# Moving the low-part subtractions of the context blocks from GpSimd to VectorE

## The chip, the cores and the metric

The kernel runs on one core of a Trainium2 chip. The time is the device time of one execution in microseconds. Engines are TensorE (PE in the profile; PEld is its weight load), VectorE (DVE), ScalarE (ACT), GpSimd (POOL) and SyncE (SP), which issues the DMAs.

## What is computed

A block of a perceiver: a cross-attention of 128 latent rows per batch (4 batches) over 2048 context rows each, then a recurrent block with ternary weights, then a mixture of 8 experts. Only the first part is touched:

```python
x = x + xattn(layernorm(x), ctx, bias, Wq, Wk, Wv, Wo)
# xattn, 16 heads of depth 32:
q = heads(x @ Wq) * 32 ** -0.5
k = heads(ctx @ Wk)
v = heads(ctx @ Wv)
out = softmax(q @ k.T + bias) @ v      # then @ Wo
```

## The kernel before, in words

The products with Wk and Wv are made in split precision. A context block `ctx_raw` (512 channels x 512 context rows, 1 MB, held as 128 x 2048 elements) is cast into a high part and a low part, both in `ctx_part`: high = cast(raw), low = raw - high. A product then takes three matmuls: high x high, high x low and low x high (L340 to L342 for keys, L361 to L363 for values). The high part is made by ScalarE (L684), the low part by a subtraction of 128 x 2048 elements.

The attention goes over 16 quads (a batch and four heads each) in 4 blocks of 32 latent rows, 64 *turns* s = 0 to 63. Meanwhile the context is visited: a visit projects one block into keys or values, in four parts, one visit per turn, turns 0 to 59. Visits 0 to 3 are done ahead of turn 0, visit s + 4 in turn s. Three buffers hold context blocks; 27 visits of `FRESH[1:]` need a newly loaded one. The visits 1 to 3 have their low part made by VectorE ahead of turn 0, the other 24 by GpSimd. `highs_after` sets the turn: the cast of a block is made behind part 2 (`HIGH_AT`) of the visit that follows the last use of its buffer, and its first reader comes two turns after the cast. This gives one subtraction in each of the turns 1, 5, 9, 10, 11, 12, 13, 17, 21, 25, 26, 27, 28, 29, 33, 37, 41, 42, 43, 44, 45, 49, 53 and 57.

What a turn does, by engine, each in this order:

- TensorE: 32 score matmuls (L438), three parts of the visit, the spread of the masked minima (L449, waits for VectorE's mask), the fourth part; in every fourth turn, from turn 4 on, also the product of the finished quad with V (L461, 128 matmuls, waits for `shift` of this turn) and the folding of the sums (L469). The scores of turn s + 1 need the four bias-adds of turn s.
- VectorE: four bias-adds with a running minimum (L565), the mask (L579, 128 x 16), the transposition of the previous turn's probabilities (L574), the reduction `shift` (L586, waits for the spread). Then, in turns 0 to 12, the sums of two weight pieces of the later ternary stage (L603, up to 128 x 1024 each), and in 26 of the turns from 14 to 55 the scaling of one piece (L627 and L630). Turns 27, 35, 39 and 43 have the pieces of 768 columns. In the turn behind a product, VectorE first inverts the sums and scales the output (L591, L598).
- ScalarE: copies of finished projections (L690, L698), the cast of a context block (L684), four exponentials (L731, wait for `shift`), the ternary conversion (L741).
- GpSimd: only the subtractions (L799), each waiting for its cast.
- SyncE: loads and stores in program order; a context block is loaded when the visit that freed its buffer is done.

Each engine works strictly in the order of its program; semaphores join them.

Of the kernel before, what the change touches and what calls it, by code (L numbers as in the profile page):

```python
# [9 lines left out]
F32 = mybir.dt.float32  # L10
# [4 lines left out]
ALU = mybir.AluOpType  # L15
# [17 lines left out]
CHUNKS = KEYS // CHUNK  # L33
# [37 lines left out]
def place_visits():  # L71

    chunk = [(h // 2, c) for kind, h, c in VISITS]
    held, used, buffer_of, fresh, freed_by = [None] * BUFFERS, [None] * BUFFERS, [], [], {}
    for i, one in enumerate(chunk):
        if one not in held:
            until = [chunk.index(other, i) if other in chunk[i:] else len(chunk) for other in held]
            at = min(range(BUFFERS), key=lambda n: (-until[n], -1 if used[n] is None else used[n]))
            fresh.append(i)
            freed_by[i] = used[at]  # L80
            held[at] = one
        at = held.index(one)
        used[at] = i
        buffer_of.append(at)
    return buffer_of, fresh, freed_by


BUFFER_OF, FRESH, FREED_BY = place_visits()
# [54 lines left out]
def perceiver_block(nc, a, out):  # L143
    with ExitStack() as life:
        def sb(name, shape, dt, stack=life):
            return stack.enter_context(nc.sbuf_tensor(name, shape, dt))

        def sem(name):
            return life.enter_context(nc.semaphore(name))

        def events(name, keys, by=1):
            return Events(sem(name), list(keys), by)
# [30 lines left out]
        ctx_raw = sb("ctx_raw", [P, BUFFERS, 2, DT, CHUNK], F32, region_i)  # L183
# [5 lines left out]
        ctx_part = sb("ctx_part", [P, BUFFERS, 2, DT, CHUNK], F32R, region_r)  # L189
# [40 lines left out]
        quads, turns = range(QUADS), range(QUADS * BLOCKS)  # L230
# [20 lines left out]
        slice_low = events("slice_low", [*((part, k) for k in range(DT) for part in ("wk", "ctx")),  # L251
                                         *(("wv", k) for k in range(DT))])
        ctx_high = events("ctx_high", FRESH[1:])
        ctx_low_v, ctx_low_g = events("ctx_low_v", FRESH[1:CHUNKS]), events("ctx_low_g", FRESH[CHUNKS:])
        key_order = [(h, c, m) for h in range(STAGES) for c in range(CHUNKS) for m in range(2)]
        value_order = [(h, c, pair) for h in range(STAGES) for c in reversed(range(CHUNKS)) for pair in range(2)]
        keys_projected, keys_copied = events("keys_projected", key_order), events("keys_copied", key_order)
# [21 lines left out]
        top_out = psum[:, 7, 2 * P:2 * P + RANGES * QUAD].rearrange("p (a j) -> p a j", a=RANGES)  # L279
        mean_out = psum[:, 7, 3 * P:3 * P + len(TERNARY)]  # L280

        def ctx_low(i):
            return (ctx_low_v if i < CHUNKS else ctx_low_g).at(i)

        def wait_for_ctx(pe, i):
            if i in FRESH:
                pe.wait_ge(*ctx_low(i))

        def visit_done(i):

# [3 lines left out]
        def parts_of(s):  # L294

            first = sum(PARTS) * (s // BLOCKS) + sum(PARTS[:s % BLOCKS])
            parts = [divmod(CHUNKS * PARTS_OF_VISIT + p, PARTS_OF_VISIT) for p in range(first, first + PARTS[s % BLOCKS])]
            return [(i, r) for i, r in parts if i < len(VISITS)]

        def highs_after(i, r):  # L300

            return [fresh for fresh in FRESH if FREED_BY[fresh] == i - 1 and r == HIGH_AT]

        def quad_weighed_in(s):

            return s // BLOCKS - 1 if s % BLOCKS == 0 and s >= BLOCKS else None
# [9 lines left out]
        def pieces_summed_in(s):  # L316
            return [u for u in (2 * s, 2 * s + 1) if 0 <= u < len(TERNARY)]
# [199 lines left out]
        def vector_attention(dve):  # L517
            own = vector_own

            def low_of_ctx(i):  # L520
                dve.wait_ge(*ctx_high.at(i))
                buffer = BUFFER_OF[i]
                dve.tensor_tensor(ctx_part[:, buffer, 1, :, :], ctx_raw[:, buffer, 1, :, :],
                                  ctx_part[:, buffer, 0, :, :].bitcast(F32),
                                  ALU.subtract).then_inc(*ctx_low_v.made(i))

            def normalise_x():
                rstd = scalars("rstd0")
# [30 lines left out]
            def add_bias(s, j):  # L559
                if (s, j) == (0, 0):  # L560
                    dve.wait_ge(*bias_placed.at(RANGES - 1, BLOCKS - 1))
                if s >= 2 and j == 0:
                    dve.wait_ge(*transposed.at(s - 2))
                dve.wait_ge(*scored.at(s, j))
                dve.tensor_tensor_reduce(  # L565
                    places_of(s)[:, j, :], psum[:, j, :], biasmap[:, (s % BLOCKS) * BANK:(s % BLOCKS + 1) * BANK], 1.0,
                    HIGHEST, ALU.add, ALU.min, top[:, s % 2, j:j + 1]).then_inc(*biased.made(s, j))

            def transpose_turn(s):
                n, block = divmod(s, BLOCKS)  # L570
                dve.wait_ge(*raised.at(s))
                if block == 0 and n:
                    dve.wait_ge(*multiplied.at(n - 1))
                dve.transpose(probT[:, :, block, :],  # L574
                              places_of(s).rearrange("p j (k r) -> p (j k) r", r=DH)).then_inc(*transposed.made(s))
# [8 lines left out]
            def join_ranges(s):  # L584
                dve.wait_ge(*top_spread.at(s))
                dve.tensor_reduce(shift[:, s % 2, :], top_out.rearrange("p a j -> p j a"), AX.X,  # L586
                                  ALU.min).then_inc(*least_made.made(s))

            def invert_sums(n):
                dve.wait_ge(*sums_folded.at(n))  # L590
                dve.reciprocal(inverse[:, :], sums_out).then_inc(*own.made())  # L591

            def finish(n):
                dve.wait_ge(*own.last())
                if n >= 1:
                    dve.wait_ge(*attended_stored.at(n - 1))
                last = attended_sb[:, DT - 1, (B - 1) * P:B * P]
                dve.tensor_tensor(oT[:, :] if n < QUADS - 1 else last, quad_out, inverse[:, :],  # L598
                                  ALU.mult).then_inc(*weighted.made(n))
# [60 lines left out]
            for s in turns:  # L660
                n = quad_weighed_in(s - 1)
                if n is not None:
                    invert_sums(n)
                    finish(n)
                for j in range(QUAD):
                    add_bias(s, j)
                mask_top(s)
                if s:
                    transpose_turn(s - 1)
                join_ranges(s)  # L670
                for u in pieces_summed_in(s):
                    sum_weights(u)
                if s == MEAN_AT:
                    find_means()
                if piece_scaled_in(s) is not None:
                    scale_weights(piece_scaled_in(s))
# [96 lines left out]
        def gpsimd_attention(pool):  # L773
            own = gpsimd_own
            pool.memset(ident[:, :], 0.0).then_inc(*own.made())
            pool.wait_ge(*own.last())
            pool.affine_select(out=ident[:, :], in_=ident[:, :], compare_op=ALU.not_equal, fill=1.0, base=0,
                               pattern=[[-1, P]], channel_multiplier=1).then_inc(*constants.made("ident"))
            pool.wait_ge(*constants.at("ident"))
            pool.memset(ones[:, :], 1.0)  # L780
            pool.memset(magic[:, 0:1], ROUND_MAGIC)
            pool.memset(magic[:, 1:2], -ROUND_MAGIC)
            pool.memset(minus_half[:, :], -0.5).then_inc(*constants.made("all"))
            pool.wait_ge(*constants.at("all"))
            for k in range(DT):
                pool.wait_ge(*slice_in[k].at("ctx"))
                pool.tensor_copy(ctx_part[:, 0, 0, k, :], ctx_raw[:, 0, 1, k, :]).then_inc(*first_ctx_high.made(k))
            rstd = scalars("rstd0")
            for t in range(B):
                pool.wait_ge(*row_measured.at(0, t))  # L790
                pool.tensor_scalar(rstd[:, t:t + 1], meanvar[:, t, 1:2], 1.0, 1e-5, ALU.mult,
                                   ALU.add).then_inc(*own.made())
                pool.wait_ge(*own.last())
                pool.tensor_tensor(rstd[:, t:t + 1], rstd[:, t:t + 1], minus_half[:, 0:1],
                                   ALU.pow).then_inc(*row_rooted.made(0, t))
            def low_of_ctx(i):
                pool.wait_ge(*ctx_high.at(i))
                buffer = BUFFER_OF[i]
                pool.tensor_tensor(ctx_part[:, buffer, 1, :, :], ctx_raw[:, buffer, 1, :, :],  # L799
                                   ctx_part[:, buffer, 0, :, :].bitcast(F32),  # L800
                                   ALU.subtract).then_inc(*ctx_low_g.made(i))

            for s in turns:
                for i, r in parts_of(s):
                    for fresh in highs_after(i, r):
                        low_of_ctx(fresh)


        def sync_attention(sp):
# [1817 lines left out]
```

## Time and profile before

| what | us |
|---|---|
| median of 3 runs | 983.29 |
| lowest and highest run | 980.52 and 991.42 |
| the profiled execution | 979.04 |
| its span in the trace | 976.6 |
| TensorE busy | 911.2 (93%) |
| VectorE busy | 623.5 (64%) |
| ScalarE busy | 502.1 (51%) |
| GpSimd busy | 215.2 (22%), of it 111.1 in L799 |

The turns lie between about 52 and 593 us of the span. Busy times are those of the one profiled execution; its own time is 2.4 us longer than its span. A busy share is an average over the whole kernel: VectorE's 64% is 84% between 100 and 200 us and 69% between 500 and 600.

### The profile page before, as it was taken

What the parts mean: (1) busy time and instruction counts of PE and PEld (TensorE: products, weight loads), DVE (VectorE), ACT (ScalarE), POOL (GpSimd) and SP (SyncE); (2) the same over time, 40 slices, a digit from 0 to 9 for tenths busy, and PEclk for the clock granted to TensorE, in tenths of its full rate; (3) what the DMA queues carried; (4) which work ended last, traced back from release to release, by engine and by line L of the source; (5) the groups of instructions that cost most, each with busy time, mean ns of one, the idle gap of its engine ahead of it and who ended that gap; (6) DMA issues with size and microseconds to landing.
All of it is one profiled execution on the core that took longest, in us unless ns stands there. A gap on an engine that the chain in (4) does not pass through costs nothing.

```text
span 976.6 us, 22422 instructions
## 1 busy us (share of the span) xinstructions
PE 911.2 (93%) x9506; PEld 750.4 (77%) x9506; DVE 623.5 (64%) x1256; ACT 502.1 (51%) x988; POOL 215.2 (22%) x216
## 2 busy tenths in 40 slices
PE   7999999999988999989999957878999999999996
PEld 5888786886866887877887833644799999999995
DVE  6379987786786678677677666775651112566551
ACT  3545666565684566675457534688410102455551
POOL 2010135011063011151101102688110201111100
PEclk8999999999998999999999978999899999999999
DMA  9435374213352113451140471000099947899930
GB/s 331 142 131 171 121 255 166 93 66 131 109 193 77 48 61 104 156 177 43 58 133 34 129 283 69 6 1 12 34 370 386 371 159 265 287 380 345 340 86 14
DMA packets 76173, 154.73 MB, mean 158 GB/s; under 512 B 5416, under 2 KB 9000, under 8 KB 75552
## 3 DMA queue, kind: packets, MB, share of 16 engines
q1 hardware_dynamic: 73952, 148.40, 43.7%
q0 software_dynamic: 2112, 4.80, 2.1%
q8 instruction: 77, 1.26, 0.5%
q14 instruction: 32, 0.26, 0.1%
HBM read 140.24 MB, written 11.90 MB: 156 GB/s over the span
## 4 chain that ended last, share of the span: by engine, by line
PE 79%; DVE 9%; POOL 5%; issue 3%; DMA 3%; SPq 0%; ACT 0%; POOLq 0%; DVEq 0%; ACTq 0%
PE psum L2031 12%; PE psum L438 7%; PE psum L340 6%; PE psum L461 6%; PE psum L361 6%; PE psum L2046 6%; PE psum L342 6%; PE psum L341 6%; PE psum L362 5%; PE psum L363 5%; DVE prob L565 3%; PE psum L2063 2%; PE psum L2065 2%; PE psum L2064 2%; DVE probT L574 1%
## 5 line engine op out<-in xcount | busy, mean ns | idle before, releaser
L731 ACT ACTIVATE prob<-prob,shift 128x512 f32<-128x512 f32 x256 | 181.8, 712 | 88.9 <-DVE shift L586 88.9
L565 DVE CUSTOM_DVE_ANT_0 prob<-psum,biasmap 128x512 f32<-128x512 f32 x256 | 161.7, 686 | 67.6 <-PE psum L438 67.3
L799 POOL TENSOR_TENSOR ctx_part<-ctx_raw,ctx_part 128x2048 fp32r<-128x2048 f32 x24 | 111.1, 4630 | 423.0 <-ACT ctx_part L684 423.0
L361 PE MATMUL psum<-wv_hi,ctx_part 128*128 128x256 f32 x512 | 150.7, 294 | 0.0
L574 DVE STREAM_TRANSPOSE probT<-prob 128x2048 f32<-128x2048 f32 x64 | 147.4, 2303 | 0.7 <-ACT prob L731 0.5
L362 PE MATMUL psum<-wv_lo,ctx_part 128*128 128x256 f32 x512 | 144.8, 283 | 0.8 <-issue 0.8
L363 PE MATMUL psum<-wv_hi,ctx_part 128*128 128x256 f32 x512 | 144.6, 282 | 0.0
L2031 PE MATMUL psum<-xT,wring 128*128 128x128 f32 (+3 forms) x1024 | 134.0, 291 | 0.4 <-ACT xT L2385 0.4
L2031 PEld LDWEIGHTS psum<-xT,wring 128*128 128x128 f32 x1024 | 130.4, 191 | 1.8 <-ACT xT L2385 0.7
L361 PEld LDWEIGHTS psum<-wv_hi,ctx_part 128*128 128x128 f32 x512 | 97.8, 191 | 26.8 <-issue 26.0
L340 PE MATMUL psum<-ctx_part,wk_hi 128*128 128x512 f32 x248 | 104.8, 423 | 0.4 <-issue 0.4
L342 PE MATMUL psum<-ctx_part,wk_lo 128*128 128x512 f32 x248 | 99.3, 400 | 0.0
L341 PE MATMUL psum<-ctx_part,wk_hi 128*128 128x512 f32 x248 | 99.3, 400 | 0.0
L362 PEld LDWEIGHTS psum<-wv_lo,ctx_part 128*128 128x128 f32 x512 | 98.0, 191 | 1.0 <-issue 1.0
L363 PEld LDWEIGHTS psum<-wv_hi,ctx_part 128*128 128x128 f32 x512 | 97.9, 191 | 0.0
L438 PE MATMUL psum<-keys_and_values,q_all 32*32 32x512 f32 x2048 | 79.2, 613 | 5.3 <-issue 5.3
L698 ACT COPY keys_and_values<-psum 128x512 f32<-128x512 f32 x64 | 36.8, 576 | 70.5 <-PE psum L363 70.5
L340 PEld LDWEIGHTS psum<-ctx_part,wk_hi 128*128 128x128 f32 x248 | 48.0, 194 | 32.2 <-issue 23.8
L690 ACT COPY keys_and_values<-psum 128x512 f32<-128x512 f32 x64 | 36.8, 577 | 67.7 <-PE psum L342 67.7
L2267 DVE TENSOR_SCALAR hidden<-psum,b 128x128 f32<-128x128 f32 (+3 forms) x64 | 23.5, 368 | 74.6 <-PE psum L2031 74.4
L461 PE MATMUL psum<-probT,keys_and_values 128*32 128x128 f32 x2048 | 62.6, 283 | 2.3 <-DVE shift L586 2.3
L461 PEld LDWEIGHTS psum<-probT,keys_and_values 128*32 128x32 f32 x2048 | 58.2, 114 | 7.4 <-DVE probT L574 3.8
(258 smaller groups left out, 1429.0 us busy)
## 6 DMA issues: line engine op xcount, KB each, us to landing
wring<-in_w SPq DMA_DIRECT2D x64, 1024.0 KB, 8.1
ctx_raw<-in_ctx_t SPq DMA_DIRECT2D x27, 1024.0 KB, 5.2
raw_piece<-in_w_gate_t SPq DMA_DIRECT2D x16, 512.0 KB, 4.1
ternary_weights<-ternary_piece SPq DMA_DIRECT2D x21, 256.0 KB, 2.2
raw_piece<-in_w_down_t SPq DMA_DIRECT2D x10, 512.0 KB, 5.0
raw_piece<-in_w_gate_t SPq DMA_DIRECT2D x8, 384.0 KB, 4.0
ternary<-ternary_weights SPq DMA_DIRECT2D x1, 2816.0 KB, 9.5
raw_piece<-in_w_i_t SPq DMA_DIRECT2D x4, 512.0 KB, 5.4
```

The lines of the kernel that those rows point to most:

```text
L340: pe.matmul(psum[:, w, :], wh, ctx_part[:, BUFFER_OF[i], 0, k, :], start=(k == 0), stop=False)
L341: pe.matmul(psum[:, w, :], wh, ctx_part[:, BUFFER_OF[i], 1, k, :], start=False, stop=False)
L342: mm = pe.matmul(psum[:, w, :], wl, ctx_part[:, BUFFER_OF[i], 0, k, :], start=False, stop=(k == DT - 1))
L361: pe.matmul(place, keys_of(0, k), wv_hi[:, k, columns], start=(k == 0), stop=False)
L362: pe.matmul(place, keys_of(0, k), wv_lo[:, k, columns], start=False, stop=False)
L363: mm = pe.matmul(place, keys_of(1, k), wv_hi[:, k, columns], start=False, stop=(k == DT - 1))
L438: mm = pe.matmul(psum[a_ * DH:(a_ + 1) * DH, j, :].rearrange("p (k r) -> p k r", k=KTILES), q_all[heads, g, tokens_in], kT(h, m)[heads, :] ...
L461: mm = pe.matmul(quad_out[j * DH:(j + 1) * DH, :], v(h, kb)[:, columns], probT[:, j * KTILES + kb, :, :], start=(kb == 0), stop=(kb == KTI ...
L565: dve.tensor_tensor_reduce(places_of(s)[:, j, :], psum[:, j, :], biasmap[:, (s % BLOCKS) * BANK:(s % BLOCKS + 1) * BANK], 1.0, HIGHEST, AL ...
L574: dve.transpose(probT[:, :, block, :], places_of(s).rearrange("p j (k r) -> p (j k) r", r=DH)).then_inc(*transposed.made(s))
L731: exp = act.activation(places_of(s)[:, j, :], places_of(s)[:, j, :], ACT.Exp, bias=shift[:, s % 2, j:j + 1], scale=-1.0, accum_out=sums[:, ...
L2031: mm = pe.matmul(psum[:, w, 0:width], wring[piece][:, k, h % 4 * P:(h % 4 + 1) * P], xT[:, q % 2, k, 0:width], start=(k == 0), stop=(k == ...
```

## The change

The 24 subtractions that GpSimd made are made by VectorE, in the turn of their cast, behind `shift` and ahead of the sums and scalings of weight pieces. The two event lists become one. GpSimd has no work left in the turns.

```diff
--- before.py
+++ after.py
@@ -251,7 +251,7 @@
         slice_low = events("slice_low", [*((part, k) for k in range(DT) for part in ("wk", "ctx")),
                                          *(("wv", k) for k in range(DT))])
         ctx_high = events("ctx_high", FRESH[1:])
-        ctx_low_v, ctx_low_g = events("ctx_low_v", FRESH[1:CHUNKS]), events("ctx_low_g", FRESH[CHUNKS:])
+        ctx_low = events("ctx_low", FRESH[1:])
         key_order = [(h, c, m) for h in range(STAGES) for c in range(CHUNKS) for m in range(2)]
         value_order = [(h, c, pair) for h in range(STAGES) for c in reversed(range(CHUNKS)) for pair in range(2)]
         keys_projected, keys_copied = events("keys_projected", key_order), events("keys_copied", key_order)
@@ -279,12 +279,9 @@
         top_out = psum[:, 7, 2 * P:2 * P + RANGES * QUAD].rearrange("p (a j) -> p a j", a=RANGES)
         mean_out = psum[:, 7, 3 * P:3 * P + len(TERNARY)]
 
-        def ctx_low(i):
-            return (ctx_low_v if i < CHUNKS else ctx_low_g).at(i)
-
         def wait_for_ctx(pe, i):
             if i in FRESH:
-                pe.wait_ge(*ctx_low(i))
+                pe.wait_ge(*ctx_low.at(i))
 
         def visit_done(i):
 
@@ -522,7 +519,7 @@
                 buffer = BUFFER_OF[i]
                 dve.tensor_tensor(ctx_part[:, buffer, 1, :, :], ctx_raw[:, buffer, 1, :, :],
                                   ctx_part[:, buffer, 0, :, :].bitcast(F32),
-                                  ALU.subtract).then_inc(*ctx_low_v.made(i))
+                                  ALU.subtract).then_inc(*ctx_low.made(i))
 
             def normalise_x():
                 rstd = scalars("rstd0")
@@ -668,6 +665,9 @@
                 if s:
                     transpose_turn(s - 1)
                 join_ranges(s)
+                for i, r in parts_of(s):
+                    for fresh in highs_after(i, r):
+                        low_of_ctx(fresh)
                 for u in pieces_summed_in(s):
                     sum_weights(u)
                 if s == MEAN_AT:
@@ -793,17 +793,6 @@
                 pool.wait_ge(*own.last())
                 pool.tensor_tensor(rstd[:, t:t + 1], rstd[:, t:t + 1], minus_half[:, 0:1],
                                    ALU.pow).then_inc(*row_rooted.made(0, t))
-            def low_of_ctx(i):
-                pool.wait_ge(*ctx_high.at(i))
-                buffer = BUFFER_OF[i]
-                pool.tensor_tensor(ctx_part[:, buffer, 1, :, :], ctx_raw[:, buffer, 1, :, :],
-                                   ctx_part[:, buffer, 0, :, :].bitcast(F32),
-                                   ALU.subtract).then_inc(*ctx_low_g.made(i))
-
-            for s in turns:
-                for i, r in parts_of(s):
-                    for fresh in highs_after(i, r):
-                        low_of_ctx(fresh)
 
 
         def sync_attention(sp):
```

VectorE in turn 1 before (the mask, the transposition, `shift`, the two sums, the first bias-add of turn 2):

```order
L579 TENSOR_TENSOR masked<-top,own_range 128x16
L574 STREAM_TRANSPOSE probT<-prob 128x64x32
L586 TENSOR_REDUCE shift<-psum 128x4
L603 TENSOR_REDUCE wsum<-raw_piece 128x1 x2
L565 ISA prob,top<-psum,biasmap 128x512
```

and in the changed kernel, whose lines behind the first edit have numbers lower by 3:

```order
L576 TENSOR_TENSOR masked<-top,own_range 128x16
L571 STREAM_TRANSPOSE probT<-prob 128x64x32
L583 TENSOR_REDUCE shift<-psum 128x4
L520 TENSOR_TENSOR ctx_part<-ctx_raw,ctx_part 128x2048
L600 TENSOR_REDUCE wsum<-raw_piece 128x1 x2
L562 ISA prob,top<-psum,biasmap 128x512
```

The subtraction (L520) stands between `shift` and the sums; everything of turn 2 is behind it.

VectorE in turn 27, where a piece of 768 columns is scaled, before:

```order
L579 TENSOR_TENSOR masked<-top,own_range 128x16
L574 STREAM_TRANSPOSE probT<-prob 128x64x32
L586 TENSOR_REDUCE shift<-psum 128x4
L627 TENSOR_SCALAR raw_piece<-raw_piece,wmean 128x768
L630 TENSOR_SCALAR raw_piece<-raw_piece 128x768
```

and in the changed kernel (its L624 and L627 are L627 and L630 of before):

```order
L576 TENSOR_TENSOR masked<-top,own_range 128x16
L571 STREAM_TRANSPOSE probT<-prob 128x64x32
L583 TENSOR_REDUCE shift<-psum 128x4
L520 TENSOR_TENSOR ctx_part<-ctx_raw,ctx_part 128x2048
L624 TENSOR_SCALAR raw_piece<-raw_piece,wmean 128x768
L627 TENSOR_SCALAR raw_piece<-raw_piece 128x768
```

The subtraction stands ahead of the scalings. On GpSimd, 24 rows of this form are gone and nothing takes their place; the orders of TensorE, ScalarE and SyncE are the same but for line numbers.

## Rows read from the trace of the kernel before

**Rows 1.** Windows, columns us and instructions busy per engine, granted clock, DMA share, GB/s

```profile
124.35:158.00 33.65, 33.13 (x472) 27.58 (x465) 29.57 (x54) 23.29 (x44) 18.45 (x4) 1.00 0.71 249
262.22:303.86 41.64, 35.22 (x471) 28.99 (x465) 32.92 (x50) 25.98 (x47) 18.35 (x4) 0.92 0.49 161
303.86:336.56 32.70, 32.35 (x424) 24.81 (x417) 22.74 (x48) 17.67 (x41) 4.62 (x1) 1.00 0.17 51
401.40:440.19 38.79, 35.51 (x471) 28.65 (x465) 29.27 (x50) 26.11 (x47) 18.82 (x4) 0.96 0.53 173
```

**Rows 2.** Lines of the subtraction, VectorE's three and GpSimd's twenty-four, min/median/max

```profile
L523 DVE TENSOR_TENSOR ctx_part<-ctx_raw,ctx_part x3: 2284/2284/2293, 18.8 to 31.2; 128x2048 fp32r<-128x2048 f32 x3
L799 POOL TENSOR_TENSOR ctx_part<-ctx_raw,ctx_part x24: 4495/4621/5037, 66.6 to 547.8; 128x2048 fp32r<-128x2048 f32 x24
```

**Rows 3.** Timeline, start and duration, one turn of VectorE

```profile
75.75 0.68 DVE L565 CUSTOM_DVE_ANT_0 prob<-psum,biasmap 128x512 f32<-128x512 f32 x1
...
78.31 0.18 DVE L579 TENSOR_TENSOR masked<-top,own_range 128x16 f32<-128x16 f32 x1
...
78.40 2.30 DVE L574 STREAM_TRANSPOSE probT<-prob 128x2048 f32<-128x2048 f32 x1
...
80.63 0.14 DVE L586 TENSOR_REDUCE shift<-psum 128x4 f32<-128x16 f32 x1
...
80.69 2.33 DVE L603 TENSOR_REDUCE wsum<-raw_piece 128x1 f32<-128x1024 f32 x2
...
82.93 0.68 DVE L565 CUSTOM_DVE_ANT_0 prob<-psum,biasmap 128x512 f32<-128x512 f32 x1
```

**Rows 4.** Timeline, the early turns, TensorE's spread and GpSimd's subtraction

```profile
65.01 0.29 PE L449 MATMUL psum<-masked,fold 128*128 128x16 f32 x2
...
66.64 4.63 POOL L799 TENSOR_TENSOR ctx_part<-ctx_raw,ctx_part 128x2048 fp32r<-128x2048 f32 x1 [48.30 <-ACT ctx_part L684]
...
72.25 0.29 PE L449 MATMUL psum<-masked,fold 128*128 128x16 f32 x2
...
154.08 1.18 PE L461 MATMUL psum<-probT,keys_and_values 128*32 128x128 f32 x35 [0.49 <-DVE shift L586]
```

**Rows 5.** Groups of VectorE lines with shapes kept apart, 75 to 570 us

```profile
L579 DVE TENSOR_TENSOR masked<-top,own_range 128x16 f32<-128x16 f32 x58 | 19.7, 339 | 2.0
...
L627 DVE TENSOR_SCALAR raw_piece<-raw_piece,wmean 128x1024 f32<-128x1024 f32 x21 | 15.5, 736 | 8.9 <-DMA raw_piece<-in_w_gate_t 4.6 <-DMA raw_piece<-in_w_f_t 1.6 <-DMA raw_piece<-in_w_down_t 1.4
...
L627 DVE TENSOR_SCALAR raw_piece<-raw_piece,wmean 128x768 f32<-128x768 f32 x4 | 10.5, 2622 | 0.0
```

**Rows 6.** Timeline of VectorE, GpSimd and TensorE, turns 26 to 28

```profile
270.69 0.69 DVE L565 CUSTOM_DVE_ANT_0 prob<-psum,biasmap 128x512 f32<-128x512 f32 x1 [2.14 <-PE psum L438]
...
277.72 4.63 POOL L799 TENSOR_TENSOR ctx_part<-ctx_raw,ctx_part 128x2048 fp32r<-128x2048 f32 x1 [4.17 <-ACT ctx_part L684]
...
282.44 0.40 PE L449 MATMUL psum<-masked,fold 128*128 128x16 f32 x2
...
283.92 4.61 POOL L799 TENSOR_TENSOR ctx_part<-ctx_raw,ctx_part 128x2048 fp32r<-128x2048 f32 x1 [1.57 <-ACT ctx_part L684]
...
284.60 4.35 DVE L627 TENSOR_SCALAR raw_piece<-raw_piece,wmean 128x768 f32<-128x768 f32 x1
...
291.50 4.50 POOL L799 TENSOR_TENSOR ctx_part<-ctx_raw,ctx_part 128x2048 fp32r<-128x2048 f32 x1 [2.98 <-ACT ctx_part L684]
...
292.02 4.01 DVE L579 TENSOR_TENSOR masked<-top,own_range 128x16 f32<-128x16 f32 x1
...
296.08 0.61 PE L449 MATMUL psum<-masked,fold 128*128 128x16 f32 x2 [6.31 <-DVE masked L579]
```

**Rows 7.** Timeline, turns 41 to 44

```profile
402.94 1.10 PE L438 MATMUL psum<-keys_and_values,q_all 32*32 32x512 f32 x18 [0.47 <-issue]
...
417.38 5.04 POOL L799 TENSOR_TENSOR ctx_part<-ctx_raw,ctx_part 128x2048 fp32r<-128x2048 f32 x1 [3.15 <-ACT ctx_part L684]
...
422.85 0.29 PE L449 MATMUL psum<-masked,fold 128*128 128x16 f32 x2
```

## Prediction, made before the changed kernel ran

> **What bounds the kernel now.** I read the windows of four groups of four turns first, then the instructions of one turn on VectorE, then the places where TensorE stands idle. An undisturbed group of four turns (29 to 32) takes 32.70 us and TensorE is busy 32.35 of them [rows 1]: TensorE is the bound. The group of turns 9 to 12 takes 33.65, that of turns 25 to 28 takes 41.64 with TensorE busy 35.22 of them, that of turns 41 to 44 takes 38.79 with 35.51 [rows 1]. So between turns 1 and 60 the bound is TensorE, except in two groups of four, and these two are where the idle time lies.
>
> How near is VectorE to being the bound? In the first twelve turns it also sums two weight pieces per turn. One such turn runs from 75.75 to 82.93, 7.18 us, without a gap [rows 3]. TensorE goes from one spread matmul (L449) to the next in 72.25 - 65.01 = 7.24 us [rows 4]. They are equal: VectorE has no room in turns 1 to 12. After turn 13 the sums are gone and VectorE waits; in turn 26 it stood idle 2.14 us before its first bias-add [rows 6].
>
> The three numbers I use later, all from [rows 3]: from the first bias-add of a turn to the end of its mask is 78.49 - 75.75 = 2.74 us; from the end of the mask to the reduction `shift` is 80.63 - 78.49 = 2.14; a pair of sums holds the engine 82.93 - 80.69 = 2.24. A spread starts 0.05 us behind its mask (296.03 and 296.08) [rows 6].
>
> **What two GpSimd subtractions did to VectorE.** At 283.92 GpSimd starts one, to 288.53. VectorE's L627, which should take about 0.56 on this size (three quarters of the 0.736 of the 1024 size [rows 5]), starts at 284.60 and takes 4.35. At 291.50 GpSimd starts the next, to 296.00, and the 16-column mask that begins at 292.02 ends at 296.03, 4.01 us instead of 0.18 [rows 3, 6]. TensorE waited 6.31 us for that mask [rows 6]. The subtraction on GpSimd thus stops some VectorE work until it ends. Over turns 3 to 60 the masks average 339 ns, not 180, and the four 768-column L627 average 2622, not about 560 [rows 5]: 58 x 0.16 = 9.2 us and 4 x 2.06 = 8.2 us, together about 17.5 us of VectorE time.
>
> The Trainium skill ("SBUF — State Buffer", Who interferes with whom) says that a VectorE instruction with two SBUF inputs, or one in a two-port mode, and a GpSimd instruction that reads SBUF exclude each other for the whole of the one that came first, while a tensor_reduce never contends. By that rule as an upper limit every one of the 24 GpSimd runs would hold VectorE, 24 x 4.62 = 111 us; the rows show a sixth of it.
>
> **The change, part by part.**
>
> *Removed:* 24 subtractions of 4.62 us on GpSimd [rows 2]. GpSimd had nothing else in these turns, so their own time is worth nothing; what goes is the blocking.
>
> *Added:* 24 subtractions on VectorE at 2.28 us [rows 2]; about 0.04 overlaps with the neighbour, so 2.24 each, 54 us in all. The readers of a low block come two turns later, so no reader waits for it. What waits is the queue behind it: the next turn's bias-adds, its mask, TensorE's spread, and in every fourth turn the product with V, which waits for `shift`. Each subtraction also waits for ScalarE's cast, which is ready when GpSimd started it.
>
> *Early turns, 1 to 13 (VectorE is full).* Turn 1: the cast allows 66.64 [rows 4]; the subtraction ends 68.88, the sums 71.12, the mask of turn 2 at 73.86, its spread at 73.91 instead of 72.25 [rows 4]: 1.7 us. In the next turns nothing is won back, as 7.18 against 7.24 leaves none. In turn 4 the product with V meets a late `shift`; in turn 12, where VectorE was already late, that cost 0.49 [rows 4], and I take 0.5. So 2.3 with 0.1 for slips. Turn 5 does the same to turns 6 to 8: 2.3. Turns 9 to 12 have one each: about 1.4 at turn 10, then a VectorE turn of 7.18 + 2.24 = 9.42 against 7.24 twice, 2.2 each, and 0.6 at the product: 6.4 (turn 10's share is smaller than turn 2's because its cast comes sooner: an estimate from turn 1's), of which 33.65 - 32.70 = 0.9 is lost already [rows 1], so 5.5. Turn 13: 0.3. Sum **+10.4**.
>
> *Turns 17, 21, 29, 33, 37, 41, 45, 49, 53, 57, one alone (and 25).* 2.24, and a wait for the cast (in turn 1 the spread is at 65.01 and the cast is ready at 66.64 [rows 4]; the reduction comes between), stand against an idle time of about 2.1. And the mask has room of its own: in turn 26 it ends at 270.69 + 2.74 = 273.4, its spread is at 282.33 - 7.24 = 275.1 [rows 4, 6], 1.7 later. Together about 3.8 against 2.24 plus at most 1 to 1.5: no cost.
>
> *Turns 26 to 28.* The cast allows 277.72 [rows 6]; subtraction to 279.96, the two scalings (2 x 0.736 less overlap, 1.4) to 281.4, mask of turn 27 at 284.1, spread 284.15, where 282.33 would do (282.44 less the 0.11 it waited): 1.8. Then `shift` at 286.3, subtraction to 288.5, scalings of the small piece 1.1, mask at 292.35; TensorE would be there at 284.15 + 7.24: 1.0 to 1.1. The product: 0.6. The group takes 32.70 + 3.5 = 36.2 instead of 41.64: **-5.4**.
>
> *Turns 42 to 44.* Same steps from 417.38 [rows 7]: mask of turn 43 at 423.75, spread due 422.85 [rows 7]: 0.95, then 1.1 and 0.6, so 2.7. Turn 41's score matmuls had a break (0.47 idle and a slow second half, 1.5 in all [rows 7]), which stays. 32.70 + 1.5 + 2.7 = 36.9 instead of 38.79: **-1.9**.
>
> *Clock.* After the 6.31 us wait the granted clock fell to 1.2 GHz (half of 2.4) for a while: 0.92 in that group, 0.96 in the group with the shorter wait, 1.00 elsewhere [rows 1]. In the changed kernel TensorE waits some nine times for 1 to 2.2 us. Waits that short don't stand in these rows; bounds are 0 and 41.64 x 0.08 = 3.3 us for each cluster of three waits. I take +1, near the lower bound because the single waits are a third of the 6.31.
>
> Sum: 10.4 - 5.4 - 1.9 + 1 = **+4.1**. The profiled execution took 979.04, so 983.1; the median of the runs is 983.29, so **987.4** on its scale, +0.4%.
>
> The Trainium skill ("Perfetto Trace Analysis", Optimizing Scalar/DVE Operations) speaks against this change: if VectorE is saturated, give work to ScalarE or even GpSimd, although the shared port may undo it. Rows 3 agree with its first half in turns 1 to 12, rows 6 with its second in turns 26 to 28. By the first half alone the sum would be +10.4 and the time 993.7.
>
> **The rivals.**
>
> 1. *Clock falls at the new waits (slower by over 1%).* Turns 10 to 12 and 26 to 28 leave TensorE idle for about a fifth of each turn. For it: the clock did fall after waiting in both groups where there was one. Against: while VectorE is the bound, a slower TensorE first eats its own idle time. It decides from two clusters of turns at 3.3 us each: 987.4 + 6.6 to 10 = 994 to 997. Chance 0.17.
>
> 2. *Late casts hold VectorE itself (slower by over 1%).* The cast waits for a ctx transfer; now all of VectorE stands behind it. In turn 26 `shift` is due at 270.69 + 2.74 + 2.14 = 275.6 and the cast is ready at 277.72, 2.1 us later [rows 6]. With 1 us more in each of eight turns: 995. The transfers seldom come later than the cast is due, so 0.08.
>
> 3. *The blocking was dearer than this execution shows (faster by over 1%).* The median lies 4.3 us above the profiled run, 991 occurred; if that is more blocking, it goes too. With half the early cost hidden: 983.29 - 7.3 - 4.3 + 5.2 = 977; it needs nearly all of the early cost hidden to pass -1%. 0.07 for under 973.5. Between 973.5 and 983, the mild form: 0.13.
>
> 4. *No effect.* GpSimd has no L799 row left in the new order, VectorE has 24 more, so the change does what it says.
>
> The forecast (983 to 993): 0.55.
>
> **Numbers.** 1% is 9.8 us, about what can be told from no change. Faster 0.07, within 0.68, slower 0.25. The range leaves out the far ends of rivals 1 and 3: 977 to 998.
>
> **What would show it.** Right: masks of 0.18 us everywhere and no L627 over 0.8; group 25 to 28 at about 36, group 41 to 44 at about 37; group 9 to 12 at about 39; TensorE waiting for the mask in turns 2, 6, 10, 11, 12. Wrong: group 9 to 12 under 36 (VectorE had room), groups 25 and 41 still near 40 (the blocking was not the cause), or a clock under 0.9 in turns 9 to 12 (rival 1).

## The result and the profile after

| | median us | lowest to highest | runs |
|---|---|---|---|
| before | 983.03 | 977.33 to 991.42 | 20 |
| changed | 989.85 | 983.48 to 993.67 | 20 |

The ratio is 1.0054 (95% interval 1.003 to 1.0078): slower by 0.5%, inside the bound of 1%. It is not the ratio of the medians (that is 1.0069); here and below it leaves out runs that lay over 1.5% above the fastest of their kernel. The forecast was 987.4, +0.4%. The profiled execution of the changed kernel took 990.17 us, its span is 988.1.

The first lines of the page, against the table of before (columns: busy us, share, instructions):

```profile
span 988.1 us, 22422 instructions
PE 914.7 (93%) x9506; PEld 750.2 (76%) x9506; DVE 658.6 (67%) x1280; ACT 502.3 (51%) x988; POOL 104.1 (11%) x192
```

GpSimd lost the 111 us of its subtractions, VectorE gained only 35 and not 24 x 2.28 = 55: most of the missing 20 us, 17.6 as shown below, had been waiting inside instructions, and the rest is the overlap of each subtraction with its neighbours. The rows that answer to [rows 1], each from the first bias-add of a group of four turns to that of the next, here for turns 1 to 4, 5 to 8, 9 to 12, 13 to 16, 25 to 28, 29 to 32 and 41 to 44:

```profile
59.44:96.48 37.04, 33.75 (x468) 27.78 (x466) 32.22 (x55) 18.86 (x44) 0.00 (x0) 1.00 0.59 198
96.48:133.88 37.40, 33.71 (x417) 24.85 (x417) 31.42 (x55) 17.66 (x41) 0.00 (x0) 0.96 0.39 131
133.88:173.06 39.18, 33.74 (x446) 27.77 (x446) 38.04 (x58) 23.36 (x44) 0.00 (x0) 0.99 0.56 186
173.06:209.60 36.54, 35.50 (x438) 26.54 (x439) 28.55 (x61) 19.77 (x43) 0.00 (x0) 0.95 0.27 87
280.70:317.16 36.46, 34.42 (x465) 28.58 (x465) 32.26 (x55) 26.09 (x47) 0.00 (x0) 0.95 0.55 174
317.16:350.04 32.88, 32.36 (x418) 24.81 (x418) 24.79 (x51) 17.67 (x41) 0.00 (x0) 1.00 0.18 55
414.88:452.40 37.52, 34.54 (x483) 28.01 (x483) 32.47 (x56) 26.09 (x47) 0.00 (x0) 1.00 0.53 171
```

In turns 9 to 12 VectorE is busy 38.04 of 39.18 us: it is the bound there. Turns 25 to 28 take 36.46 instead of about 41.7, turns 29 to 32 are as before. The same measure, first bias-add to first bias-add, worked out from the starts of L565 (later L562 or the like) in each trace:

| turns | 1-4 | 5-8 | 9-12 | 13-16 | 21-24 | 25-28 | 41-44 | 49-52 |
|---|---|---|---|---|---|---|---|---|
| before | 32.9 | 32.2 | 33.7 | 34.6 | 36.9 | 41.7 | 38.8 | 35.5 |
| changed | 37.0 | 37.4 | 39.2 | 36.5 | 38.4 | 36.5 | 37.5 | 35.3 |
| difference | +4.2 | +5.2 | +5.5 | +2.0 | +1.5 | -5.2 | -1.3 | -0.1 |

The groups left out differ by 0.4 at most. The sum is +11.8 in these two executions, though the medians differ by 6.8: single runs of one kernel lie up to 14 us apart, and the profiled run of before was one of the shorter ones (979.04), while that of the changed kernel (990.17) lies at its median.

The early loss, on VectorE (start, duration, idle before and its releaser), turns 1 and 2:

```profile
64.33 0.13 DVE L583 TENSOR_REDUCE shift<-psum 128x4 f32<-128x16 f32 x1
65.36 2.29 DVE L520 TENSOR_TENSOR ctx_part<-ctx_raw,ctx_part 128x2048 fp32r<-128x2048 f32 x1 [0.89 <-ACT ctx_part L684]
67.57 2.34 DVE L600 TENSOR_REDUCE wsum<-raw_piece 128x1 f32<-128x1024 f32 x2
69.83 0.68 DVE L562 CUSTOM_DVE_ANT_0 prob<-psum,biasmap 128x512 f32<-128x512 f32 x1
...
72.38 0.17 DVE L576 TENSOR_TENSOR masked<-top,own_range 128x16 f32<-128x16 f32 x1
```

and on TensorE, the spreads of turns 2 and 12 and the two breaks ahead of turns 5 and 9:

```profile
72.61 0.40 PE L446 MATMUL psum<-masked,fold 128*128 128x16 f32 x2 [1.41 <-DVE masked L576]
...
95.26 1.15 PE L435 MATMUL psum<-keys_and_values,q_all 32*32 32x512 f32 x31 [1.39 <-issue]
...
131.19 0.65 PE L466 MATMUL psum<-fold,sums 128*32 128x32 f32 x32 [2.18 <-issue]
...
165.44 0.40 PE L446 MATMUL psum<-masked,fold 128*128 128x16 f32 x2 [2.04 <-DVE masked L576]
```

The chain is the forecast one: a wait of 0.89 for the cast, 2.2 for the subtraction, the sums behind it, a late mask, TensorE waiting 1.41 and later 2.04. The two rows with "issue" were not forecast: TensorE stood although no other engine held it. The DMA records of the same trace show what came just before. A queue of its own, q8, carries the program's instructions in pieces of 16 KB, one about every 10 us in the turns. One such transfer started at 92.91 and one at 128.79, and TensorE went on 2.35 and 2.40 us later (the view of 128.7 to 128.9 us):

```profile
q8 instruction: 1, 0.02, 30.1%
```

Turn 27, which answers to [rows 6]. Its mask before:

```profile
280.49 1.90 DVE L579 TENSOR_TENSOR masked<-top,own_range 128x16 f32<-128x16 f32 x1
```

and in the changed kernel:

```profile
301.06 0.17 DVE L576 TENSOR_TENSOR masked<-top,own_range 128x16 f32<-128x16 f32 x1
...
303.44 2.27 DVE L520 TENSOR_TENSOR ctx_part<-ctx_raw,ctx_part 128x2048 fp32r<-128x2048 f32 x1
305.63 0.61 DVE L624 TENSOR_SCALAR raw_piece<-raw_piece,wmean 128x768 f32<-128x768 f32 x1
```

```profile
301.29 0.40 PE L446 MATMUL psum<-masked,fold 128*128 128x16 f32 x2 [1.78 <-DVE masked L576]
```

The mask takes 0.17 instead of 1.90, the scaling 0.61 instead of 4.35. And the groups that answer to [rows 5] (mean ns after the bar and the busy time):

```profile
L576 DVE TENSOR_TENSOR masked<-top,own_range 128x16 f32<-128x16 f32 x58 | 10.2, 175 | 2.0
L624 DVE TENSOR_SCALAR raw_piece<-raw_piece,wmean 128x768 f32<-128x768 f32 x4 | 2.4, 607 | 0.0
```

From 339 to 175 ns and from 2622 to 607: 9.5 and 8.1 us, 17.6 in all.

### The profile page after: what moved, and what is told of

Its sections match the earlier page's. It is cut to its first block, busy times and chain, and to the rows that moved or that the text cites. A ratio compares the mean times of both kernels' runs of the same rounds, so it can differ in the third digit from the quotient of the medians.

```text
span 988.1 us, 22422 instructions
## 1 busy us (share of the span) xinstructions
PE 914.7 (93%) x9506; PEld 750.2 (76%) x9506; DVE 658.6 (67%) x1280; ACT 502.3 (51%) x988; POOL 104.1 (11%) x192
## 4 chain that ended last, share of the span: by engine, by line
PE 73%; DVE 12%; POOL 5%; issue 4%; DMA 3%; ACT 1%; SPq 0%; POOLq 0%; DVEq 0%; ACTq 0%
PE psum L2020 12%; PE psum L435 6%; PE psum L458 6%; PE psum L2035 6%; PE psum L337 6%; PE psum L358 5%; PE psum L338 5%; PE psum L339 5%; PE psum L359 4%; PE psum L360 4%; DVE prob L562 4%; DVE probT L571 2%; PE psum L2052 2%; PE psum L2054 2%; PE psum L2053 2%
## 5 line engine op out<-in xcount | busy, mean ns | idle before, releaser
L562 DVE CUSTOM_DVE_ANT_0 prob<-psum,biasmap 128x512 f32<-128x512 f32 x256 | 161.6, 686 | 40.3 <-PE psum L435 39.7
L435 PE MATMUL psum<-keys_and_values,q_all 32*32 32x512 f32 x2048 | 81.3, 622 | 7.3 <-issue 7.3
L520 DVE TENSOR_TENSOR ctx_part<-ctx_raw,ctx_part 128x2048 fp32r<-128x2048 f32 x27 | 61.7, 2286 | 11.1 <-ACT ctx_part L684 11.1
## 6 DMA issues: line engine op xcount, KB each, us to landing
ternary<-ternary_weights SPq DMA_DIRECT2D x1, 2816.0 KB, 10.2
```

What stands on the lines that cost most here:

```text
L435: mm = pe.matmul(psum[a_ * DH:(a_ + 1) * DH, j, :].rearrange("p (k r) -> p k r", k=KTILES), q_all[heads, g, tokens_in], kT(h, m)[heads, :] ...
L562: dve.tensor_tensor_reduce(places_of(s)[:, j, :], psum[:, j, :], biasmap[:, (s % BLOCKS) * BANK:(s % BLOCKS + 1) * BANK], 1.0, HIGHEST, AL ...
```

## The experiments

Theory: two effects of opposite sign. VectorE has no room in turns 1 to 12, so subtractions there delay the masks; from turn 13 on what costs is the blocking by GpSimd, in two clusters of turns.

**Half of the change each.** The subtractions are given to VectorE by a condition on the visit i (19 is the visit whose cast falls into turn 13):

```diff
+        on_vector = lambda i: i < CHUNKS or i < 19      # first run
+        on_vector = lambda i: i < CHUNKS or i >= 19     # second run
+        on_vector = lambda i: i < CHUNKS or i in (32, 33, 34, 48, 49, 50)   # third run
```

> Only the six subtractions of turns 1, 5, 9, 10, 11 and 12 are on VectorE, the other 18 on GpSimd. Theory (VectorE is full while it sums weight pieces; later the blocking by GpSimd is what costs): +10 us against the kernel before, ratio 1.010; turns 9 to 12 take about 39 us from first bias-add to first bias-add of turn 13, turns 25 to 28 still about 41. Rival (blocking by GpSimd costs as much in the early turns too, so that moving it is free): within 3 us of before.

Measured 993.67 (median of 6), ratio 1.0104 (1.0054 to 1.0154). Turns 9 to 12 took 39.7, turns 25 to 28 took 42.0. The theory's +10 us is met, the rival's 3 are not. Its trace shows more than that: turns 1 to 16 took 14.7 us longer than in the trace of before.

> The other half: turns 1 to 12 on GpSimd, the 18 subtractions from turn 13 on VectorE. Theory: -7 us, ratio 0.993; turns 25 to 28 take about 36.4 us instead of 41.6, turns 41 to 44 about 37 instead of 38.8, all lone turns as before. Rival (the gain in turns 25 to 28 of the change is an accident of where its earlier delays put the transfers): no gain, ratio 1.00.

Measured 975.02 (12 runs), ratio 0.9928 (0.9898 to 0.9958). Turns 1 to 4, 9 to 12, 25 to 28 and 41 to 44 of its trace:

```profile
59.80:92.67 32.87, 32.87 (x466) 27.76 (x466) 30.11 (x55) 18.82 (x44) 4.62 (x1) 1.00 0.62 202
...
124.83:158.61 33.78, 32.98 (x446) 27.24 (x445) 29.58 (x56) 23.28 (x44) 18.45 (x4) 1.00 0.70 243
261.71:298.57 36.86, 33.28 (x465) 27.58 (x465) 32.27 (x56) 25.92 (x47) 0.00 (x0) 1.00 0.54 173
396.35:433.08 36.73, 34.39 (x483) 27.88 (x479) 32.47 (x56) 26.09 (x47) 0.00 (x0) 1.00 0.54 173
```

GpSimd is at work in the first two (4.62, 18.45 us) and not in the last two, which take 36.9 and 36.7. The expected -7 us is there, and the gain did not need the early delays.

> Only the six subtractions of turns 26, 27, 28, 42, 43 and 44 are on VectorE. Theory: all of the late gain is in these, so the same -7 us as with 18 of them, ratio 0.993. Rival (every lone GpSimd subtraction blocks something that counts): clearly less gain than with all 18 moved, under 4 us.

Measured 974.77 (12 runs), ratio 0.9926 (0.9894 to 0.9958): six moved subtractions gain what 18 do. The other twelve late ones block nothing that counts, though on GpSimd they still lengthen single masks to 0.33 to 0.46 us.

**The change again, for the breaks.**

> The change itself once more, for a second trace. Theory A (the extra 4 us of turns 1 to 8 beyond the forecast are breaks of TensorE's instruction supply at fixed places of the program that come once it waits there): breaks of 1 to 2 us at the first scores of turns 5 and 9 again, ratio 1.006. Theory B (they were chance): turns 1 to 4 take 35 us, turns 5 to 8 take 34.6 from first bias-add to first bias-add, and the time is 3 us lower.

Measured 987.05 (12 runs), ratio 1.004 (1.0006 to 1.0075). Turns 1 to 4 took 37.5, turns 5 to 8 took 37.1, so theory B falls. TensorE's breaks came back, 1.68 us at the scores of turn 5 and 1.24 at the folding ahead of turn 9. In the run with the early half the first was absent (turns 1 to 4 took 36.2) and the second was there, 1.84. In no trace in which GpSimd made the early subtractions did either occur. So they go with the early delays, but not each time.

The 14 traces say what the breaks are bound to. Between 52 us and turn 60 they hold 82 breaks of 0.4 us or more that no engine released. In 80 of them TensorE went on 2.19 to 2.55 us behind the start of a 16 KB transfer on the instruction queue; in the other two, both in one run (the change with its subtractions last, below), 2.8 and 3.4 us behind. The transfers come 3 to 22 us apart, so this is not chance; the reading that fits is that TensorE had used up its instructions and waited for the next piece. Near turns 5 and 9 the transfer started 2.1 to 4.0 us behind the start of the product with V where there was a break, and 0.2 to 2.3 us behind it where there was none. What makes the transfer start later when VectorE is late stays open, and no experiment moved a transfer by itself.

**Behind the scalings and sums.** The subtraction moved to the end of VectorE's turn:

```diff
                 if piece_scaled_in(s) is not None:
                     scale_weights(piece_scaled_in(s))
+                for i, r in parts_of(s):
+                    for fresh in highs_after(i, r):
+                        if on_vector(fresh):
+                            low_of_ctx(fresh)
```

> As the run with the 18 late subtractions on VectorE, but each stands behind the scalings of its turn and not ahead of them. Theory (in turns 26 and 42 VectorE stands waiting for the cast while scalings of 1.4 us could be made): 1 to 1.5 us saved in each of the two groups, so about 972.5, ratio 0.990; turns 25 to 28 take about 35. Rival (the scalings were hidden anyway): 975, ratio 0.993.

Measured 974.5 (6 runs), ratio 0.9873 (0.9837 to 0.9908). Turns 25 to 28 took 34.8 and not 36.9, as expected; turns 41 to 44 took 36.9 where they had taken 36.7, so nothing was saved there. The medians, 974.5 here and 975.0 there, are from different chips (the kernel before had 984.2 there and 985.7 here) and don't separate the theory's 972.5 from the rival's 975. The ratio, taken against the kernel before on the same chip, speaks for the theory: the rival's 0.993 lies outside its interval.

> The change with each subtraction behind the sums and scalings of its turn. Theory (VectorE is full in turns 1 to 12, and only the waiting for the casts, about 0.9 us in turn 1, 0.5 in turn 5, 0.9 in turn 9, can be saved): the early cost shrinks by 1.5 to 2.5 us, and another 2 come from turns 26 and 42: 983 to 985, ratio 1.001. Rival (the place in the turn decides the early cost): early cost gone, under 978.

Measured 986.44 (12 runs), ratio 1.0016 (0.999 to 1.0042). The ratio is what the theory said, the median is 1.4 us above its 983 to 985. Turns 1 to 4, 5 to 8 and 9 to 12 took 37.6, 35.1 and 39.3 instead of 37.0, 37.4 and 39.2 in the change: only the second group is shorter, so little of the early cost depends on the place in the turn: 1.7 us, or 2.3 against the second trace of the change, as the theory said. Turns 25 to 28 fell to 34.9.

**VectorE's room, given back.** The sums read 64 columns of each piece:

```diff
-                dve.tensor_reduce(wsum[:, u:u + 1], piece_place(u), AX.X, ALU.add,
+                dve.tensor_reduce(wsum[:, u:u + 1], piece_place(u)[:, 0:64], AX.X, ALU.add,
```

> The change with sums over only 64 columns of each piece and weight matrix (most of the summing is left out, so the ternary scales and what follows are not the reference's). Theory: VectorE then has about 2 us free in each of turns 1 to 12, so the early cost falls from 13 us to 3 (turns 9 to 12, with one subtraction each, keep about 1 to 2 us): ratio to before 0.996; turns 1 to 4 and 5 to 8 take 32.3 to 33, turns 9 to 12 take 33 to 35. Rival (TensorE's breaks and the waits for the casts make the early cost, not the full VectorE): these groups still take 36 us or more.

The whole run took 1616.68 us: with other ternary scales the later layers do other work (the largest group of matmuls, L2031 before and L2038 here, has 4096 instead of 1024). So it can't be compared, and the ratio that was expected has no meaning. The turns can. Turns 1 to 4, 5 to 8 and 9 to 12:

```profile
59.10:91.97 32.87, 32.87 (x467) 27.76 (x466) 24.42 (x56) 18.84 (x44) 0.00 (x0) 1.00 0.60 204
91.97:124.13 32.16, 32.16 (x418) 24.81 (x418) 24.31 (x56) 17.66 (x41) 0.00 (x0) 1.00 0.45 150
124.13:157.44 33.31, 32.56 (x446) 27.18 (x445) 30.82 (x59) 23.29 (x44) 0.00 (x0) 1.00 0.74 252
```

With all subtractions on VectorE (GpSimd 0.00) and short sums the early cost is gone, breaks included: 32.87, 32.16 and 33.31, the values of before. VectorE without room is what the whole early cost hangs on, the breaks included.

**What the blocking hangs on.** All subtractions on GpSimd as before, but the mask's factor lies in PSUM, so that the mask has one SBUF input:

```diff
+        own_range_out = psum[:, 7, 3 * P - RANGES:3 * P]
-                                  own_range[:, :].rearrange("p (a o) -> p a o", o=1).broadcast_to([P, RANGES, QUAD]),
+                                  own_range_out.rearrange("p (a o) -> p a o", o=1).broadcast_to([P, RANGES, QUAD]),
-            dve.tensor_reduce(own_range[:, :], ident...
+            dve.tensor_reduce(own_range_out, ident...
```

> The kernel before, all 24 subtractions on GpSimd, but the mask reads its factor own_range from PSUM, so that it has one SBUF input instead of two. Theory (a GpSimd subtraction stops a VectorE instruction that reads two SBUF operands): all 64 masks take 0.2 us, also while GpSimd subtracts, the one of turn 28 too; the scalings of 768 columns still take 4 to 5 us in turns 27 and 43. Turns 25 to 28 take 37 to 38 instead of 41.6, and the time is 3 to 5 us lower, ratio 0.996. Rival (the masks are stopped by the writes of GpSimd, or by its load on SBUF): masks of 1 to 4 us remain and nothing changes.

Measured 970.24 (6 runs), ratio 0.9848 (0.9806 to 0.9889): 15 us below before, where 3 to 5 were expected. Turns 25 to 28, then GpSimd's and VectorE's instructions in turns 26 to 28:

```profile
260.81:293.49 32.68, 32.68 (x465) 27.57 (x465) 23.63 (x51) 25.87 (x47) 18.78 (x4) 1.00 0.60 194
```

```profile
275.35 4.66 POOL L806 TENSOR_TENSOR ctx_part<-ctx_raw,ctx_part 128x2048 fp32r<-128x2048 f32 x1 [4.52 <-ACT ctx_part L691]
281.18 4.93 POOL L806 TENSOR_TENSOR ctx_part<-ctx_raw,ctx_part 128x2048 fp32r<-128x2048 f32 x1 [1.18 <-ACT ctx_part L691]
```

```profile
277.77 0.17 DVE L582 TENSOR_TENSOR masked<-top,psum 128x16 f32<-128x16 f32 x1
...
280.37 0.13 DVE L589 TENSOR_REDUCE shift<-psum 128x4 f32<-128x16 f32 x1
280.43 0.60 DVE L630 TENSOR_SCALAR raw_piece<-raw_piece,wmean 128x768 f32<-128x768 f32 x1
```

The mask of turn 27 runs at 277.77 in the middle of a GpSimd subtraction (275.35 to 280.01) and takes 0.17. So the scaling starts at 280.43, ahead of the next subtraction at 281.18, and takes 0.60. In the kernel before the mask had waited 1.9 us, and so the scaling started 0.7 us *behind* the next subtraction and waited 3.8; that put the next mask into a third one [rows 6]. I had expected the scalings of turns 27 and 43 to stay blocked. They were not: one collision of 1.7 us made the other two, and the group took 32.68, the undisturbed time, with TensorE busy throughout. The rival's masks of 1 to 4 us don't occur; all 64 take 170 to 172 ns. Turns 41 to 44 gained less and took 36.3: turn 43's mask and scaling are free too (1.28 and 4.94 us before), but turn 41 took 10.8 us, with a break of 1.1 and a stretch at half clock behind it.

> The change (all subtractions on VectorE) with the mask's factor read from PSUM. Theory (the gain of the mask from PSUM is the end of the blocking by GpSimd, and here GpSimd has nothing to block with): no difference to the change, ratio to before 1.004, turns 25 to 28 at 36.4. Rival (a mask with a PSUM operand is of use in itself, by 0.2 us or more per turn): 5 us or more below the change.

Measured 990.45 (12 runs), ratio 1.0055 (1.0023 to 1.0086); turns 25 to 28 took 37.0. The same as the change. The PSUM operand is of no use in itself; its gain is the end of the blocking.

> All subtractions on GpSimd, mask factor from PSUM, once more on this chip. Theory (the 1.9 us block of the mask in turn 27 is what pushes the scaling, the bias-adds and the next mask into further GpSimd subtractions; without it none of them collides): turns 25 to 28 take 32.7 again and turns 41 to 44 about 34 to 36 (with the break of turn 41), ratio 0.985 to 0.988. Rival (the 32.7 was luck of one execution): 36 or more there, ratio above 0.992.

Measured 969.02 (6 runs), ratio 0.987 (0.9826 to 0.9914); turns 25 to 28 took 32.68 again, turns 41 to 44 took 36.3 (with a break of 1.1 us in turn 41 and the clock at 0.95), a little over the 34 to 36 expected. This version beats both kernels: about -14 us to before, and on this chip -18 to the change.

**The kernel before, twice more.**

> The kernel before, for a second trace, since its first one is of a run of 979.0 us while its median is 983 to 986. Theory A (the 4 to 6 us lie in deeper collisions of GpSimd subtractions with VectorE in turns 25 to 28 or 41 to 44): these groups take longer than 41.6 and 38.8 where the run is slower. Theory B (they lie in TensorE's breaks and half-clock stretches anywhere): these groups are the same and others differ.

> A third trace of the kernel before. As above: theory A says turns 25 to 28 or 41 to 44 differ between the three traces by what their times differ, theory B says that other groups do.

One run each, 979.33 and 976.77 us. Turns 25 to 28 took 41.5 and 41.6 (41.7 in the first trace), turns 41 to 44 took 38.6 and 37.5 (38.8), turns 21 to 24 took 35.1 twice (36.9), turns 49 to 52 took 35.8 and 36.9 (35.5). The big collision comes every time with the same size. Neither run was one of 983 or more, so in which turns a median run of before is longer than a traced one stays open. The clocks on record point to theory B: of 27 further runs of before on one chip, the ten with a mean granted clock of 0.970 or more averaged 980.1 us, the nine with 0.966 or less 987.4.

## Why the prediction was right, point by point

The mechanism was right on both sides, and so was the late gain in size. The early cost was forecast about 7 us too small for the traces, and part of the near hit is luck; both are told at the sum.

- *The bound before.* The prediction puts the idle time into two groups of four only. The table above has more: turns 13 to 16, 21 to 24 and 49 to 52 took 34.6, 36.9 and 35.5 us, each with a break of TensorE, and in turns 21 to 24 the granted clock was 0.95 and not 1.00. These groups hardly changed the forecast, since they stood in both kernels.
- *VectorE has no room in turns 1 to 12, a turn with both takes 9.42 us.* Right. The steps between first bias-adds in turns 10 and 11 were 9.38 and 9.38. Turns 9 to 12 lost 5.5 us, the forecast figure, and 6.1 in the second trace. The short sums took the early cost away altogether.
- *Turns 1 to 8: 2.3 + 2.3.* Too small in every trace: +4.2 and +5.2 in the first, +4.6 and +4.9 in the second. The waits were as forecast (spread of turn 2 8.81 us behind that of turn 1 instead of 7.24, so 1.6 against 1.7; 0.49 at the product); the rest are TensorE's breaks of 1.2 to 2.2 us at the starts of turns 5 and 9 and, in the second group, the clock at 0.96. The term for slips was 0.1 per group and should have been 2 to 3.
- *Turn 13: 0.3.* It was 2.0 in this trace and 1.8 in the second; the granted clock was 0.95 in this group, where before it was 1.00, and turn 13's scores had the same break in all three traces. The clock is most of the rest.
- *Turns 26 to 28: -5.4, group of 36.2.* Right: 36.46, 36.2 and 36.9 in three traces. In the second trace its parts were the forecast ones: 1.52, 0.91 and 0.49 us of waiting at the spreads of turns 27 and 28 and at the product, for 1.8, 1.0 to 1.1 and 0.6. In the first only the 1.78 at turn 27 was there; behind it the clock was at half from 301.8 to 305.3 us (0.95 in the group), TensorE was busy 34.42 us instead of about 32.4, and the other two waits didn't show. No mask was over 0.18 in either.
- *Turns 42 to 44: -1.9, group of 36.9.* Right within 0.6: 37.5 and 37.3.
- *Lone turns: no cost.* Right: turns 17 to 20 and 29 to 40 are the same within 0.2, and 18 late subtractions gained what six did.
- *Clock +1.* Right in sign for these groups, too small in size: the granted clock was 0.96 and 0.99 in two early groups and 0.95 in turns 13 to 16 and 25 to 28, by the prediction's own working (time of the group times what is missing of 1.00) up to 5.5 us. Over the whole span both kernels have 0.97, so rival 1 did not happen. The prediction also lets the clock fall after the 6.31 us wait; in the trace it was at half from 293.7 to 300.6 us, so it fell during the wait, which ended at 296.1.
- *The sum.* +4.1 forecast. The halves measured alone are 1.0104 and 0.9928, +10.2 and -7.1 us on 983, where the forecast had +10.4 and -7.3; together +3.1, and the change was measured at +5.3 (1.0054) and +3.9 (1.004). This agreement is in part luck. In the two traces of the change, turns 1 to 16 cost 16.9 and 17.4 us more than in the trace of before, not 10.4, while turns 25 to 28 and 41 to 44 gave back 6.5 and 7.0, as forecast (7.3). The profiled execution was forecast at 983.1 and took 990.17, 7 us more. The medians are nearer to each other than the traces because the three traced runs of before (979.04, 979.33 and 976.77) are 4 to 6 us shorter than its median, and those of the change (990.17, 987.36) are not. The prediction added 4.3 us for this to its sum. That a median run of the change has nothing of the kind hides most of the 7 us that were left out of the early cost.
- *Rival 3, the blocking is dearer than this execution shows.* Wrong for the change. But the blocking was worth more than the 7 us that the late half collected: about 14 by the mask from PSUM. In turns 25 to 28 VectorE's own subtractions cost 3.8 to 4.2 us (36.5 and 36.9 against 32.7). How much of the rest is their price is not settled: with the subtractions behind the scalings the ratio was 0.9873, which the intervals don't separate from 0.9848 and 0.987. The prediction took up the collisions of turns 27 and 28 one by one; they were one and its two consequences.

On the mechanism, the Trainium skill ("SBUF — State Buffer", Who interferes with whom) says that a VectorE instruction with at most one SBUF input outside the two-port modes doesn't contend with GpSimd. The masks bear it out on both sides: up to 4.01 us with two SBUF inputs, 0.17 with one, while GpSimd subtracts. The scalings, which have one tensor as input, were held too (4.35 us for 0.6); no run here moved their operand or changed their mode.

## What to carry to other kernels

When a small instruction of one engine shows a mean twice its median, look at what GpSimd does in the long ones: here a 16-column multiply took 4 us, and changing where its operand lies gained 14 us, while moving 111 us of GpSimd's work cost 5. When TensorE stands with no releaser, look at the instruction queue in the DMA records. Before moving work to an engine with a low average share, measure its period against the bound's stage by stage: VectorE's 64% was 7.18 against 7.24 us in the first twelve turns and two idle microseconds a turn later on. A collision shifts what follows it, so its price is read from the whole group of turns and not from the sum of its long instructions.

## What was not expected of the hardware

- One blocked 16-column mask (1.90 us) set off blocks of 4.35 and 4.01 us; without the first the others did not occur, although GpSimd still subtracted four times in that group (18.78 us).
- TensorE breaks with no releaser end 2.2 to 2.55 us behind the start of a 16 KB transfer on the instruction queue, in 80 of 82 cases: as far as the traces show, TensorE waits for its next piece of code there.
- Breaks of 1.2 to 2.2 us came at the starts of turns 5 and 9 only in kernels whose VectorE was late there, in 9 of 10 places of five traces; breaks at the scores of turns 13, 21 and 49 came in every trace of every kernel, and at turn 41 in 10 of 14.
